# A two-pass mixture-of-experts and attention kernel: the shared expert transposed by chunks of four tiles, and the steps between the passes placed anew among its slices

## What is computed

```python
x = x + 0.5 * ffn(layernorm(x))      # pass 0
x = x + attention(layernorm(x))      # 16 heads of 8, causal, 2 x 1024 tokens, 128 channels
x = x + 0.5 * ffn(layernorm(x))      # pass 1

def expert(h, g, u, d): return (silu(h @ g.T) * (h @ u.T)) @ d.T     # hidden width 352
def ffn(x):
    probs = softmax(x @ wr.T + rb)                # 7 routed experts
    scores, idx = top_k(probs, 2); scores /= scores.sum()
    return expert(x, shared) + sum over the 2 chosen e of score_e * expert(x, e)
```

## Time and profile before

| | |
|---|---|
| median of 3 runs | 547.82 us (542.69 to 549.03) |
| the profiled execution | 545.02 us |
| its span, first to last instruction | 543.2 us |
| busy in the span | PE 502.0, DVE 386.7, ACT 318.9, POOL 271.3 us |
| granted TensorE clock, mean | 0.981 of full |

### The profile page before, as it was taken

The page is one execution under the profiler, slowest core; times in us unless marked ns, Lnnn a source line. Parts: engine busy times, 40 slices in busy tenths (PEclk is TensorE's granted clock), DMA queues, the critical chain, the costliest instruction groups (busy, mean ns, idle before and its releaser), DMA issues.

```text
span 543.2 us, 12861 instructions
## 1 busy us (share of the span) xinstructions
PE 502.0 (92%) x4312; PEld 364.6 (67%) x4312; DVE 386.7 (71%) x1032; ACT 318.9 (59%) x690; POOL 271.3 (50%) x417
## 2 busy tenths in 40 slices
PE   5988899999998899999999999999898899899994
PEld 2888898998855554444444445356447899899994
DVE  4795654558479999898989899874455774454835
ACT  4662444457544577878787878687665344344632
POOL 8399898676485411222313130302348898844440
PEclk9998999999999999999999999899999999899998
DMA  8932414232753634150505050300000141422213
GB/s 272 309 90 55 120 60 124 68 113 61 220 172 103 210 81 160 26 179 7 184 2 185 2 184 1 107 1 4 2 11 30 44 91 57 129 78 90 86 40 116
DMA packets 35053, 52.63 MB, mean 97 GB/s; under 512 B 6000, under 2 KB 23920, under 8 KB 34352
## 3 DMA queue, kind: packets, MB, share of 16 engines
q1 hardware_dynamic: 27632, 39.03, 24.6%
q0 software_dynamic: 4480, 9.25, 5.1%
q10 hardware_dynamic: 2880, 3.55, 2.1%
HBM read 31.93 MB, written 28.00 MB: 110 GB/s over the span
## 4 chain that ended last, share of the span: by engine, by line
PE 50%; DVE 33%; issue 8%; POOL 3%; DMA 3%; SPq 1%; ACTq 1%; ACT 1%; DVEq 0%; POOLq 0%
DVE mxp L1884 24%; PE psum L961 10%; PE psum L944 5%; PE psum L1784 5%; PE psum L922 5%; PE psum L923 5%; PE psum L924 5%; PE psum L1743 5%; PE psum L1674 2%; DMA b_p<-in_attn_c_proj_b 2%; PE psum L1684 2%; PE psum L984 1%; POOL z_rows L1248 1%; PE psum L1825 1%; DVE act L1080 1%
## 5 line engine op out<-in xcount | busy, mean ns | idle before, releaser
L1884 DVE TENSOR_REDUCE mxp<-psum 128x1 f32<-128x512 f32 (+3 forms) x320 | 179.4, 627 | 15.8 <-PE psum L1684 11.9
L1940 ACT ACTIVATE probs<-psum 128x512 f32<-128x512 f32 x256 | 136.5, 601 | 35.0 <-PE psum L1743 34.0
L1035 ACT ACTIVATE silu<-psum 128x352 f32<-128x352 f32 x107 | 49.6, 464 | 100.2 <-PE psum L924 68.4
L1080 DVE TENSOR_TENSOR act<-silu,psum 128x352 f32<-128x352 f32 x107 | 55.5, 519 | 67.1 <-ACT silu L1035 39.7
L1271 POOL DMA_INDIRECT y_rows<-ys,to_row x76 | 74.3, 977 | 51.3 <-DVE ys L1116 25.5
L1743 PE MATMUL psum<-queries,keys 32*128 32x512 f32 (+7 forms) x384 | 98.1, 416 | 1.0 <-ACT probs L1940 1.0
L961 PE MATMUL psum<-wall_f,at 128*128 (+1 forms) x648 | 91.7, 278 | 2.8 <-DVE x L1118 1.6
L1989 POOL TENSOR_SCALAR_AFFINE_SELECT probs<-probs 128x512 f32<-128x512 f32 x48 | 29.6, 638 | 122.6 <-ACT probs L1940 122.6
L961 PEld LDWEIGHTS psum<-wall_f,at 128*128 128x128 f32 x648 | 82.0, 194 | 3.6 <-issue 2.9
L1743 PEld LDWEIGHTS psum<-queries,keys 32*128 32x128 f32 (+1 forms) x384 | 50.9, 186 | 35.1 <-ACT probs L1940 16.8
L1784 PE MATMUL psum<-probs,vg 128*32 128x512 f32 (+2 forms) x640 | 73.0, 530 | 0.0
(11 more groups left out here) (253 smaller groups left out, 853.6 us busy)
## 6 DMA issues: line engine op xcount, KB each, us to landing
z_rows<-q_stack SPq DMA_DIRECT2D x12, 682.5 KB, 5.5
keys<-k_stack SPq DMA_DIRECT2D x32, 128.0 KB, 5.2
queries<-q_stack SPq DMA_DIRECT2D x8, 512.0 KB, 4.9
zg_early<-z_rows SPq DMA_DIRECT2D x44, 65.0 KB
yc<-y_rows SPq DMA_DIRECT2D x10, 256.0 KB, 2.7
zg_late<-z_rows SPq DMA_DIRECT2D x32, 65.0 KB
yc<-y_rows ACTq DMA_DIRECT2D x6, 256.0 KB, 3.0
wall_f<-in_ffn_rd SPq DMA_DIRECT2D x1, 1344.0 KB, 16.4
```

The costliest lines, as they stand in the source:

```text
L1884: e.tensor_reduce(dst, scores, AX.X, ALU.max).then_inc(K.A["taken"], 1)
L1940: e.activation(strip_of(K, w)[:, j, :], slot(K, u, d, n)[:, 0:strip_width(w)], ACT.Exp, scale=SCALE).then_inc(K.A["ex"], 1)
```

## The change

- The shared expert runs by chunk c and slice k of the hidden width (128, 128, 96): weights stationary, 512 tokens as columns, so that `act` comes out transposed. Transposes and `at` copies of shared jobs go. 12 shared jobs take the place of 16; a place "-" behind each three is empty. `down` is 4 matmuls for each job, accumulated over the three slices, and x is updated once for each chunk, 512 wide. In pass 1 nine shared jobs (chunks 0 to 2) precede the routed ones and three (chunk 3) follow; the product of the last routed job goes ahead of the first of these.
- Of the norm, POOL keeps the power alone. Variance plus epsilon and the product -mean * rstd (`norm_mr_dve`) go to DVE.
- x is loaded as chunk 0, chunk 1, and the rest. In pass 0, statistics of chunks 2 and 3 go from the start to the front of step 1, behind `places`, and the power for them into `sort_pool`, in the place of two pauses. Their z, transposes, high and low parts and logits move to steps 1 to 6. The low parts of the shared weights go from DVE to POOL.
- In pass 1, transposes of chunks 2 and 3 go to step 4, their logits to step 5, `places` to step 8 (PE) and behind step 7 (DVE). SP reads the row numbers of two batches at once at job 10.

```diff
 BEFORE = (TT, 11)
+SHARED = [("s", (c, k)) if k < 3 else ("-", c) for c in range(NCH) for k in range(TPC)]
+JOBS = [SHARED[:b] + [("r", j) for j in range(NJ)] + SHARED[12:12 + TT - b] for b in BEFORE]
+JOBS[1] += [("-", NCH - 1)] * (NJ + TT - len(JOBS[1]))
...
 def norm_stats_dve(K, k, c):
+    e.wait_ge(K.NS[k]["mv"], VARIANCE * c + TPC + 1)
+    e.tensor_scalar(K.var_e[:, v, :], K.mv[:, v, :, 1], LN_EPS, None, ALU.add).then_inc(K.NS[k]["mv"], 1)
 def norm_rstd_pool(K, k, c):
+    e.wait_ge(K.NS[k]["mv"], VARIANCE * (c + 1))
+    e.tensor_tensor(K.rstd[:, v, :], K.var_e[:, v, :], K.half_neg[:, :], ALU.pow).then_inc(K.NS[k]["rstd"], 1)
+def norm_mr_dve(K, k, c):
     if z_on_act(k, c):
+        e.wait_ge(K.NS[k]["rstd"], c + 1)
+        e.scalar_tensor_tensor(K.mr_neg[:, v, :], K.mv[:, v, :, 0], -1.0, K.rstd[:, v, :], ALU.mult, ALU.mult)
 def norm_z_act(K, k, c):
-    e.wait_ge(K.NS[k]["rstd"], 4 * c + 4)
+    e.wait_ge(K.NS[k]["mr"], sum(z_on_act(k, before) for before in range(c + 1)))
...
 def up_pe(K, f, q, base):
+        if kind == "s":
+            h0, width = HT[k]
+            dst = bank(K, b)[0:width, :]
+            e.matmul(dst, K.wall[:, hi + h0:hi + h0 + width], zh, start=True, stop=False)
+            e.matmul(dst, K.wall[:, lo + h0:lo + h0 + width], zh, start=False, stop=False)
+            ins = e.matmul(dst, K.wall[:, hi + h0:hi + h0 + width], zl, start=False, stop=True)
 def down_pe(K, f, q, base):
+    if kind == "s":
+        e.wait_ge(s["act"], jobs_done(f, q + 1, "act"))
+        for t in range(TPC):
+            cols = slice(t * P, (t + 1) * P)
+            ins = e.matmul(bank(K, Y_BANK)[:, cols], shared_act(K, c, k)[:, cols],
+                           K.wall_f[0:HT[k][1], DN + k * EMB:DN + (k + 1) * EMB],
+                           start=(k == 0 and t == 0), stop=(k == 2), skip_group_check=True)
 def yev_dve(K, f, q):
+        x = K.x[:, n[0] * TPC:(n[0] + 1) * TPC, :].rearrange("p t e -> p (t e)")
+        e.scalar_tensor_tensor(x, bank(K, Y_BANK), 0.5, x, ALU.mult, ALU.add).then_inc(s["yev"], 1)
...
+NORM_FOR_PAUSE = {(0, TT + 1): 2, (0, 2): 3}
 def sort_pool(K, f, g):
-    if g % TT > 0:
+    if (f, g) in NORM_FOR_PAUSE:
+        norm_rstd_pool(K, f, NORM_FOR_PAUSE[f, g])
+    elif g % TT > 0:
         pause_pool(K, f == 1 and t < HALF)
...
 FRONT_DVE (pass 0)
-    1: (("places", 0),)
+    1: (("places", 0), ("stats0", 2), ("stats0", 3), ("mr0", 2), ("mr0", 3))
 BEHIND_ACT (pass 0)
-    {2 * k + 2: (("weights", m),) ...
+    {1: (("z0", 2),), 2: (("z0", 3),), 2 * k + 3: (("weights", m),) ...
 BEHIND_DVE (pass 0)
-    2 * k + 3: (("weights_lo", m),) ...
+    2 * k + 4: (("weights_lo", m),) ...
 BETWEEN_DVE
-    [{0: (("lo0", 2),), 1: (("lo0", 3),)}, {4: (("router", (1, 0)),), 6: (("places", 1),)}]
+    [{3: (("lo0", 2),), 4: (("lo0", 3),)}, {4: (("norm_lo", 2), ("norm_lo", 3)), 5: (("router", (1, 0)),)}]
 BETWEEN_PE
-    [{0: (query, tr0 2, places 0), 1: (tr0 3), 3: (logits0 2), 4: (logits0 3)}, {1: (proj_tr 2, 3), 4: (logits 2, 3), 6: (places 1)}]
+    [{0: (query, places 0), 3: (tr0 2), 4: (tr0 3), 5: (logits0 2), 6: (logits0 3)}, {1: (proj_tr 2, 3), 4: (norm_tr 2, 3), 5: (logits 2, 3)}]
```

More of the change, by code:

```diff
@@ L469, in place_memory @@
     K.NS = [{n: sem(f"n{k}_{n}") for n in
-                  ("bn", "mv", "rstd", "z", "tr", "hi", "lo")} for k in range(3)]
+                  ("mv", "rstd", "mr", "z", "tr", "hi", "lo")} for k in range(3)]
     K.RS = {n: sem(f"r_{n}") for n in ROUTE_STEPS}
@@ L1008, in ffn_pe @@
         if step < NQ:
-            if f == 0 or step > 0:
+            if JOBS[f][step][0] != "-" and (f, step) not in ((1, 0), BEHIND_ROUTED):
                 up_pe(K, f, step, bases.get(step, 0))
@@ L1061, in ffn_act @@
             rows_hi_act(K, f, b)
-        if step < NQ and (f == 0 or step > 0):
+        if step < NQ and JOBS[f][step][0] != "-" and (f, step) not in ((1, 0), BEHIND_ROUTED):
             silu_act(K, f, step)
@@ L1225, in ffn_dve @@
             rows_lo_dve(K, f, b)
-        if step < NQ:
+        if step < NQ and JOBS[f][step][0] != "-" and (f, step) != BEHIND_ROUTED:
             act_dve(K, f, step)
@@ L1326, in rows_load_sp @@
             e.wait_ge(K.rows_known, 2 * f + (1 if b == 0 else 2))
-        _, rows = K.nc.values_load_multi_w_load_instructions(
-            K.rows_at[0:1, j0:j0 + n], engines=(mybir.EngineType.SP,), min_val=0, max_val=SORTED - P,
-            skip_runtime_bounds_check_because="a region's start and whole tiles behind it, all within the sorted rows")
+        if j0 == WHOLE:
+            two = n + BATCHES[b + 1][1]
+            _, known = K.nc.values_load_multi_w_load_instructions(
+                K.rows_at[0:1, j0:j0 + two], engines=(mybir.EngineType.SP,), min_val=0, max_val=SORTED - P,
+                skip_runtime_bounds_check_because="a region's start and whole tiles behind it, all within the sorted rows")
+            rows, known = known[:n], known[n:]
+        elif known:
+            rows, known = known, []
+        else:
+            _, rows = K.nc.values_load_multi_w_load_instructions(
+                K.rows_at[0:1, j0:j0 + n], engines=(mybir.EngineType.SP,), min_val=0, max_val=SORTED - P,
+                skip_runtime_bounds_check_because="a region's start and whole tiles behind it, all within the sorted rows")
         if j0 in (0, WHOLE):
@@ L2297, in late_dve @@
         norm_lo_dve(K, 0, c)
+    elif step == "stats0":
+        K.nc.vector.wait_ge(K.ld_x[2], 16)
+        norm_stats_dve(K, 0, c)
+    elif step == "mr0":
+        norm_mr_dve(K, 0, c)
     elif step == "query":
@@ L2327, in late_dve @@
         norm_stats_dve(K, 1, c)
+    elif step == "n_mr":
+        norm_mr_dve(K, 1, c)
+    elif step == "mr":
+        norm_mr_dve(K, 2, c)
     elif step == "n_lo":
```

266 lines of the change are left out of this document (152 added, 114 removed).

## The result

The changed kernel takes 548.66 us for 547.94 (medians of 20 runs each). The ratio of the times is 1.0084, 95% interval 1.0048 to 1.012; it leaves disturbed runs out (one of 967 us among them), so it is not the quotient of the two medians. The kernel is slower by 0.8%, some 4.6 us, well within 2%. The profiled execution took 548.54 us for 545.02, a span of 546.8 us for 543.2. That is +3.5 us, the prediction's sum to the tenth, but it is made up otherwise.

What follows compares the result with a forecast made beforehand. It took POOL's scatter chain to bound job 10 of pass 0, slots and POOL pass 1's, then the end. Terms +5.0 + 1.0 - 0.4 + 1.1 + 0.3 - 3.5 = +3.5 on 545.0: 548.5 profiled, forecast 550 us (542 to 558).

Steps and rivals of the forecast that it cites:

- What bounds pass 0: Job 10 of pass 0: PE waits for POOL's chain of 32 scatters, so PE time saved before 80.6 is worth nothing.
- The stall, +5.0: Pass 0, step 1: DVE idles 7 us at two `mr0` awaiting POOL's powers, making job 10 5.0 us later.
- the clock, +1.0: Pass 0, job 10: after PE's longer wait one job runs at the lower clock level, +1.0 us.
- The start: Before the first scatter: slots of half 0 come 0.3 us earlier, 1.3 more if the bias landed with the logits.
- The attention's start, -0.4: Statistics to z of chunks 2 and 3: one POOL operation for four, DVE gets the others; 0.4 us less.
- Pass 1, +1.1 and +0.3: Pass 1 to job 10: longer chain to half 1's slots, POOL starts 1.1 us later; lower PE clock adds 0.3.
- The tail, -3.5: End of kernel: three shared jobs for five tiles save 4.2 us of PE, wider operations return 0.7; -3.5 us.
- they wait for each other: Rival at the tail: late y rows or wide jobs waiting for one another give -0.8 for -3.5, 553 us; chance 0.12.
- the stall is covered: Rival in pass 0: half 1's slots still come before POOL is free, so no stall cost; 544 us, chance 0.28.
- Stall plus low clock: Rival: PE stays at the lower clock through shared jobs, job 10 at +9, slow jobs after; 560 us, chance 0.1.
- that rule: GpSimd contends with two-input DVE instructions; an idle DVE shortens pass 0's fourth scatter by 0.6 us, sum 547.9 for 548.5.

Runs made afterwards that it cites:

- the version with all edits: Changed kernel with norm powers, `mr0`, first `n_mr`, tail's wide up and pass 1's logits reordered, router bias on its own semaphore; ratio to the kernel before 0.9951.

## Why the prediction was right

It gave 550.0 us (542 to 558), most likely no difference over 2%. The whole is right; of its terms three were mis-sized, and their errors (-3.6, +1.8 and +1.6 us) cancel. That the sum fits to the tenth is luck, the more so as the attention alone swings by 7 us between executions.

- **What bounds pass 0** is the step that failed: "What it waits for is a chain on POOL", "Whatever PE saves ahead of 80.6 is therefore lost". Job 10's wait ended with PE's filler: it follows PE's arrival by 3.67 us in every execution with it, and the rows would have allowed it about 2.4 us sooner. I had the row of the filler and its 2.32 us in the earlier trace rows and took for granted that the rows came after it.
- **The stall, +5.0, with the clock, +1.0**: the mechanism and its places are right (4.60 and 2.14 us for 5 and 2; PE idle 7.56 us; slots of half 1 at 52.5 for a forecast of 53.6; POOL's loads +4.5). At job 10 it came to +2.4, by another way than I gave: not POOL's rows but PE itself came 2.4 us later, behind its stand of 7.56 us, and POOL's 4.5 us stayed hidden behind the filler. The slow job was there, but as the second routed one (64.52) and not behind job 10. Part of POOL's lateness is longer scatters: that of 53.30 takes 2.69 us beside DVE's weight split, and from there to the first y scatter it is 26.8 us for 25.4.
- **The start** was 0.8 us earlier for 0.3: the bias had landed. Over the other executions that was luck.
- **The attention's start, -0.4**: wrong sign, +1.4. I counted the operations that left POOL, not what is queued ahead of the one that went to DVE: a mixing of 1.14 us, a sum, a product and a copy. With one entry moved, all of it came back at that place.
- **Pass 1, +1.1 and +0.3**: job 10 came 1.4 us later against the slots of half 0; by the last routed job it was 1.1. Right, though within the swing (118.8 to 121.0 us to that job in the three executions of the kernel before's order, 120.1 to 124.2 in the seven of the changed one's). Of the chain's 1.7 us from slots to slots 1.0 was the logits behind an up.
- **The tail, -3.5**: -1.9. The three wide jobs were priced as PE's share of a full pipeline (5.7 us for 9.9). At the end nothing follows them: from 531.72 to the x update at 539.22 it is 7.5 us, product and down of the third slice included, and it begins only behind the last routed down. The rival "they wait for each other" had the mechanism, at -0.8 too small a gain.
- **The rivals**: "the stall is covered" was half true, by filler on PE and not by slack on POOL. "Stall plus low clock": the clock did fall behind the stall (0.75 of full in the window of the earlier trace rows, 1.00 before), but it was back to full by 39 us, and its second fall, at the second routed job, lies within the 0.9 us that PE's ten jobs took longer.
- **The Trainium skill**, "GPSIMD Engine Reference", section "1. Specifications", on the interface shared with VectorE: at 26.92 the fourth scatter took 0.96 us with DVE standing still, 1.57 beside the split, as that rule has it.

In sum +2.4, +1.4, about +0.5 to the end of the attention, +1.1 and -1.9: +3.5. The 4.6 us of the ratio lie 1 us above it, within the swing of the stages.

## What to carry to other kernels

Where an engine seems to wait for a chain elsewhere, look at the last thing it did before it went on: filler that ends exactly there hides slack. Measure the job against the engine's own arrival and against the issue of its loads, over several executions: the distance that never changes points to what binds. When a small operation moves from an idle engine to a busy one, its price is the queue ahead of it at that place, not its length. At the end of a kernel, price a job by its latency from first operation to last, not by its share of a full pipeline.

## What was not expected of the hardware

- The attention, with nearly the same instructions, took 246.7 to 254.0 us in 14 profiled executions, and its length follows the granted clock of PE in that stretch: 0.98 to 0.99 of full in the five shortest, 0.95 to 0.97 in the nine others, 0.95 in the longest. That is nearly half of the spread of 538 to 554 us between runs of the kernel before.
- PE's clock behind a wait. In pass 1 of the version with all edits, PE stood 1.60 us for the z rows and 0.92 us once more, and then lost 1.6 us in two jobs, with matmuls of 0.49 us for 0.32 (the lower of the clock's two levels, 1.2 for 2.4 GHz); with 1.3 us of filler in its place it lost nothing. Of the 13 executions without that filler, eight show such slow jobs there: seven of the eight in which PE's first stand there was longest (1.25 to 3.64 us), and one of the other five (0.89 to 1.17 us), that of the kernel before. With the second stand counted in, the two groups overlap: executions without a slow job stood 1.2 to 2.4 us, those with one 1.9 to 4.6. So a slow job is likely there, not certain.
- Scatters on POOL, 0.96 us alone, take 1.5 to 2.7 us beside DVE's weight splits: in the changed kernel 1.52, 1.97, 1.93 and 2.69, 4.3 us more than alone, where the kernel before had 1.57, 1.63 and 1.72, 2.0 us more. The length follows from the split's end: each of these seven ends 0.84 us behind the end of the split (53.30 + 2.69 = 55.99 for a split of 53.53 + 1.62 = 55.15), and so do all the others that a split stretched in the 14 executions. Such a scatter waits for the whole split; the split takes no longer for it.
